# Reordering the lead-in of a two-layer convolution and attention kernel: large loads first, a joint weight product spread over five banks, and the group norm's products placed inside it

## The reference, cut to what matters

```python
def _gn(v, G=32, eps=1e-5):
    g = v.reshape(B_, G, C_ // G, H_, W_)
    m = jnp.mean(g, axis=(2, 3, 4), keepdims=True)
    s = jnp.var(g, axis=(2, 3, 4), keepdims=True)
    return ((g - m) / jnp.sqrt(s + eps)).reshape(v.shape)

# layer 0: depthwise 3x3 convolutions of the normalised image
value = _dwconv(x, w_v, b_v, 1)
query = _dwconv(x, w_q, b_q, 1)
key = _dwconv(x, w_k, b_k, STRIDE)      # stride 2
off = _dwconv(x, w_off1, b_off1, STRIDE)
...
# layer 1
mid = jax.nn.silu(xn @ fc1_w + fc1_b) @ fc2_w + fc2_b
...
o = o + mid
o = o @ proj_w + proj_b

x = x + _L0_conv_ref(_gn(x), ...)
x = x + _L1_conv_ref(_gn(x), ...)
```

## Time and profile before

| | us |
|---|---|
| median of 3 runs | 2768.92 |
| the profiled execution, whole | 2791.05 |
| its span | 2789.2 |
| PE busy | 2687.2 (96%) |
| DVE busy | 1978.9 (71%) |
| ACT busy | 1169.6 (42%) |
| mean granted TensorE clock | 0.969 |

### The profile page before, as it was taken

One profiled execution on the slowest core, in us unless ns is written; L12 is line 12 of the kernel. 1 busy time (PEld: TensorE's weight loads), 2 busy tenths in 40 slices (PEclk: granted clock), 3 DMA queues, 4 the chain that ended last, 5 costly groups with the idle time before them and its releaser, 6 DMA issues.

```text
span 2789.2 us, 36724 instructions
## 1 busy us (share of the span) xinstructions
PE 2687.2 (96%) x14382; PEld 2444.5 (88%) x14382; DVE 1978.9 (71%) x2513; ACT 1169.6 (42%) x2035; POOL 655.7 (24%) x219
## 2 busy tenths in 40 slices
PE   6998799999999999999999999999999999999999
PEld 4556799999998899999998899999998899999998
DVE  4988785988887685988887685988887534434343
ACT  3432465444442465444442366444442253333332
POOL 0020142222232043222223042322224033211210
PEclk8998899999999999999999999999999999999999
DMA  5257643343338642334337743333346632112110
GB/s 224 59 151 246 207 129 83 105 114 114 102 108 258 215 132 75 103 106 115 123 91 231 241 140 84 102 102 102 104 124 204 232 101 70 44 44 57 44 43 30
DMA packets 208249, 345.52 MB, mean 124 GB/s; under 512 B 24272, under 2 KB 191824, under 8 KB 205392
## 3 DMA queue, kind: packets, MB, share of 16 engines
q1 hardware_dynamic: 182048, 309.87, 34.3%
q10 hardware_dynamic: 21552, 14.05, 3.7%
q0 software_dynamic: 4480, 19.27, 2.4%
HBM read 239.59 MB, written 103.56 MB: 123 GB/s over the span
## 4 chain that ended last, share of the span: by engine, by line
PE 74%; DMA 7%; issue 7%; DVE 5%; POOL 4%; ACT 2%; SPq 0%; ACTq 0%; DVEq 0%; POOLq 0%
PE bank L780 16%; PE bank L781 16%; PE bank L782 16%; PE bank L826 3%; PE bank L985 3%; PE bank L987 3%; PE bank L986 3%; PE bank L1008 3%; PE bank L1176 3%; DMA r_scr<-rr 3%; POOL rq L702 2%; PE bank L1162 2%; DVE AC L2391 1%; PE bank L1120 1%; POOL ro L706 1%
## 5 line engine op out<-in xcount | busy, mean ns | idle before, releaser
L1750 ACT ACTIVATE S<-bank,b1p 128x448 f32<-128x448 f32 x336 | 212.4, 632 | 819.5 <-PE bank L782 752.5
L2391 DVE SCALAR_TENSOR_TENSOR AC<-XV,wfold,AC 128x1568 f32<-128x1568 f32 x288 | 530.0, 1846 | 11.5 <-ACT AC L1782 8.9
L780 PE MATMUL bank<-SH,W2H 128*128 128x448 f32 x1008 | 389.9, 387 | 0.2
L780 PE MATMUL bank<-XRH,W1H 128*128 128x448 f32 x1008 | 376.8, 374 | 1.3 <-ACT S L1750 1.3
L781 PE MATMUL bank<-SL,W2H 128*128 128x448 f32 x1008 | 374.0, 371 | 0.0
L782 PE MATMUL bank<-SH,W2L 128*128 128x448 f32 x1008 | 373.7, 371 | 0.0
L781 PE MATMUL bank<-XRL,W1H 128*128 128x448 f32 x1008 | 373.2, 370 | 0.0
L782 PE MATMUL bank<-XRH,W1L 128*128 128x448 f32 x1008 | 371.9, 369 | 0.0
L702 POOL TENSOR_TENSOR rq<-qn,nhalf 112x32 f32<-112x32 f32 x28 | 181.9, 6498 | 481.0 <-DVE qn L2330 481.0
L2360 DVE TENSOR_TENSOR SL<-S,SH 128x448 fp32r<-128x448 f32 x336 | 207.1, 618 | 87.7 <-ACT SH L1753 87.7
L706 POOL TENSOR_TENSOR ro<-on,nhalf 112x32 f32<-112x32 f32 x28 | 180.2, 6434 | 298.7 <-DVE on L2351 298.6
(11 more groups left out here) (227 smaller groups left out, 5169.0 us busy)
## 6 DMA issues: line engine op xcount, KB each, us to landing
XV<-in_xp SPq DMA_DIRECT2D x36, 870.0 KB, 6.9
XC<-in_xp SPq DMA_DIRECT2D x13, 1682.0 KB, 9.2
CQ<-q_scr SPq DMA_DIRECT2D x28, 672.0 KB
CX<-in_x SPq DMA_DIRECT2D x28, 672.0 KB, 5.2
x_scr<-CX SPq DMA_DIRECT2D x28, 672.0 KB, 5.7
X<-x_scr SPq DMA_DIRECT2D x28, 672.0 KB, 4.2
V<-v_scr SPq DMA_DIRECT2D x28, 672.0 KB, 7.3
Y<-x_scr SPq DMA_DIRECT2D x28, 672.0 KB
```

Source lines behind the costliest of these rows:

```text
L780: mm(o, wh, xh, start=first, stop=False)
L1750: fn(S[:, j % 2, :], bank[j % 2][:, 0:T], ACT.Silu, bias=b1p[:, j:j + 1]).then_inc(s["s_s"], 1)
L2391: stt(o, XV[h][:, ky:ky + HR, kx:kx + W], wfold[:, kind, k, 3 * ky + kx:3 * ky + kx + 1], o, ALU.mult, ALU.add).then_inc(s["va"], 1)
```

## The change

It touches the head of the lead-in and one order on DVE.

```diff
         CONSTS = 13
+        WB = (5, 6, 1, 2, 3)
@@ block.sync
+            sp.dma_start(projw[:, :, :].rearrange("p k c -> p (k c)"), d["proj_w"]).then_inc(s["stg_ld1"], 16)
+            sp.dma_start(fc2w[:, :, :].rearrange("p k c -> p (k c)"), d["fc2_wT"]).then_inc(s["stg_ld1"], 16)
+            for k in range(KC):
+                sp.dma_start(XP[k][:, :, :], xpad_v[0, :, k, :, :]).then_inc(s[f"x0_ld{k}"], 16)
+            sp.dma_start(grp[:, :, :], d["grp"]).then_inc(s["grp_ld"], 16)
             for dst, src in [
...
                 sp.dma_start(dst.ap(), src).then_inc(s["const_ld"], 16)
-
-            sp.dma_start(projw[:, :, :].rearrange("p k c -> p (k c)"), d["proj_w"]).then_inc(s["stg_ld1"], 16)
-            sp.dma_start(fc2w[:, :, :].rearrange("p k c -> p (k c)"), d["fc2_wT"]).then_inc(s["stg_ld1"], 16)
-            for k in range(KC):
-                sp.dma_start(XP[k][:, :, :], xpad_v[0, :, k, :, :]).then_inc(s[f"x0_ld{k}"], 16)
-            sp.dma_start(grp[:, :, :], d["grp"]).then_inc(s["grp_ld"], 16)
@@ block.tensor
-            pe.wait_ge(s["const_ld"], CONSTS * 16)
-            pe.wait_ge(s["stg_ld1"], 32)
-            for j in range(JC):
-                if j >= 2:
-                    pe.wait_ge(s["set_lo"], j - 1)
+            def joint_weight(j):
+
+                if j >= len(WB):
+                    pe.wait_ge(s["set_lo"], j - len(WB) + 1)
                 for k in range(KC):
-                    last = mm(bank[5 + j % 2][:, 0:C], fc2w[:, k, j * P:(j + 1) * P], projw[:, k, :],
+                    last = mm(bank[WB[j % len(WB)]][:, 0:C], fc2w[:, k, j * P:(j + 1) * P], projw[:, k, :],
...
+            pe.wait_ge(s["stg_ld1"], 32)
+            for j in range(9):
+                joint_weight(j)
...
-            gn_groups(0, bank[4], bank[7])
+            gn_groups(0, bank[4], bank[7], lambda: joint_weight(9))
+            joint_weight(10)
+            joint_weight(11)
+            pe.wait_ge(s["const_ld"], CONSTS * 16)
@@ front_taps
+                    if m == 0:
+                        pe.wait_ge(s["set_lo"], JC)
@@ block.scalar
-            act.wait_ge(s["const_ld"], CONSTS * 16)
...
+            joint_high(0, 9)
             act.wait_ge(s["kvq_ld"], 16)
             fn(WKVH[:, :, :], kvw[:, :, :], ACT.Copy).then_inc(s["w_h"], 1)
-            fn(WPH[:, :, :], projw[:, :, :], ACT.Copy).then_inc(s["w_h"], 1)
+            joint_high(9, 10)
...
+            joint_high(10, JC)
...
+            act.wait_ge(s["const_ld"], CONSTS * 16)
             act.wait_ge(s["gn_cf"], 2)
-            front_centre(0)
+            front_centre(0, slice(0, 1))
             front_diag(0)
+            front_centre(0, slice(1, 2))
             front_centre(1)
             front_diag(1)
+            fn(WPH[:, :, :], projw[:, :, :], ACT.Copy).then_inc(s["w_h"], 1)
@@ block.vector
-            dve.wait_ge(s["const_ld"], CONSTS * 16)
-            dve.tensor_reduce(wsum[:, :, :], wconv[:, :, :, :], AX.X, ALU.add)
...
-                order = [(k, c, i) for k in range(2) for i in range(1, 9) for c in (1, 0)]
+                order = [(0, c, i) for c in (1, 0) for i in range(1, 9)]
+                order += [(1, c, i) for i in range(1, 9) for c in (1, 0)]
...
-            for j in range(4):
-                w2_low(j)
-            chunk_stats(0)
-            w2_low(4)
-            w2_low(5)
-            chunk_stats(1)
-            w2_low(6)
-            w2_low(7)
-            chunk_stats(2)
+            w2_low(0)
+            chunk_stats(0)
+            w2_low(1)
+            w2_low(2)
+            chunk_stats(1)
+            for j in range(3, 6):
+                w2_low(j)
+            chunk_stats(2)
             dve.wait_ge(s["x0bn"], STRIPS)
-            gn_coefs(0, bank[4], bank[7], ((w2_lows(8, JC),), (wkv_low,), ()))
+            gn_coefs(0, bank[4], bank[7], ((w2_lows(6, 9),), (weight_sums, w2_lows(9, 10), wkv_low), ()))
+            w2_low(10)
+            w2_low(11)
             small_conv(0, 48)
```

More of the change, by code:

```diff
@@ L1372, in _, with joint_high @@
             fn = act.activation
-            act.wait_ge(s["const_ld"], CONSTS * 16)
             def f(ap):
                 return ap.bitcast(F32)
-            for j in range(JC):
-                act.wait_ge(s["set_w2"], j + 1)
-                fn(W2H[:, j, :], bank[5 + j % 2][:, 0:C], ACT.Copy).then_inc(s["stg_h"], 1)
+            def joint_high(first, last):
+                for j in range(first, last):
+                    act.wait_ge(s["set_w2"], j + 1)
+                    fn(W2H[:, j, :], bank[WB[j % len(WB)]][:, 0:C], ACT.Copy).then_inc(s["stg_h"], 1)
+            joint_high(0, 9)
             act.wait_ge(s["kvq_ld"], 16)
             fn(WKVH[:, :, :], kvw[:, :, :], ACT.Copy).then_inc(s["w_h"], 1)
-            fn(WPH[:, :, :], projw[:, :, :], ACT.Copy).then_inc(s["w_h"], 1)
+            joint_high(9, 10)
             act.wait_ge(s["gn_s1"], 1)
@@ L1393, in _, with front_centre @@
                 last.then_inc(s["bord"], 2)
-            def front_centre(k):
+            joint_high(10, JC)
+            def front_centre(k, which=slice(0, 2)):
                 centre = XP[k][:, 1:2 + 2 * (HK - 1):2, 1:2 + 2 * (WK - 1):2]
@@ L1399, in front_centre @@
                     act.wait_ge(s["ktp"], HEAD + 2)
-                for dst, conv, sg in ((OA2[:, k, :], 3, "o0"), (KA2[:, k % 2, :], 2, "k0")):
+                for dst, conv, sg in ((OA2[:, k, :], 3, "o0"), (KA2[:, k % 2, :], 2, "k0"))[which]:
                     fn(dst.rearrange("p (r w) -> p r w", w=WK), centre, ACT.Identity,
@@ L2034, in w2_low @@
                 dve.wait_ge(s["stg_h"], j + 1)
-                tt(W2L[:, j, :], bank[5 + j % 2][:, 0:C], f(W2H[:, j, :]), ALU.subtract).then_inc(s["set_lo"], 1)
+                tt(W2L[:, j, :], bank[WB[j % len(WB)]][:, 0:C], f(W2H[:, j, :]), ALU.subtract).then_inc(s["set_lo"], 1)
             def w2_lows(first, last):
@@ L2096, in centre_columns, with weight_sums @@
                     last.then_inc(s["set_ctr"], 1)
-            for j in range(4):
-                w2_low(j)
-            chunk_stats(0)
-            w2_low(4)
-            w2_low(5)
-            chunk_stats(1)
-            w2_low(6)
-            w2_low(7)
+            w2_low(0)
[4 more added lines that the diff above has]
+            for j in range(3, 6):
+                w2_low(j)
             chunk_stats(2)
             dve.wait_ge(s["x0bn"], STRIPS)
-            gn_coefs(0, bank[4], bank[7], ((w2_lows(8, JC),), (wkv_low,), ()))
+            def weight_sums():
+                dve.wait_ge(s["const_ld"], CONSTS * 16)
+                dve.tensor_reduce(wsum[:, :, :], wconv[:, :, :, :], AX.X, ALU.add)
+            gn_coefs(0, bank[4], bank[7], ((w2_lows(6, 9),), (weight_sums, w2_lows(9, 10), wkv_low), ()))
+            w2_low(10)
+            w2_low(11)
             small_conv(0, 48)
```

## The result

| | changed kernel | kernel before, on the same chip | ratio [95% interval] |
|---|---|---|---|
| first timing | 2759.22 | 2771.17 | 0.9934 [0.9916, 0.9951] |
| again | 2759.14 | 2779.68 | 0.9930 [0.9914, 0.9947] |
| a third time | 2765.31 | 2782.27 | 0.9951 [0.9932, 0.9971] |

The two columns of times are medians. By the ratios the changed kernel is faster by 18.3, 19.5 and 13.6 us in the three comparisons; the intervals run from 8 to 24 us and all hold 17. (The medians differ by 12.0, 20.5 and 17.0. The 2771.17 counts the three runs of the kernel before that I started from; without them its mean is 2776.37 and that of the changed kernel 2757.91, which gives the 0.9934.) I had forecast 9.4. That the median of 2759.22 stands beside my 2759.5 is luck: the kernel before, 2768.92 in the runs that I started from, took 2776 to 2782 beside the changed one.

What follows compares the result with a forecast made beforehand. PE is busy 96% of the span, but the head is bound by PE and DVE waiting in turns. Savings of 9.2 at the statistics and 0.2 later, none lost, take 2768.9 to 2759.5 us; range 2755.5 to 2764.5.

Steps and rivals of the forecast that it cites:

- Transfers, `fc2w`: Head: with large transfers first, `fc2w` is issued at 1.20, 6.12 us earlier, and lands at 10.4 instead of 16.53.
- The first chunk is issued at 1.7 and lands 16.3 later, at 18.0: Head: DVE waits for this image chunk until 18.0, so the statistics are gathered at 33.4 instead of 42.62, saving 9.2.
- PE idle for 3.8, clock at 1.2 GHz: Ahead of the group norm's first product: PE idles 29.6 to 33.4, so that product takes 3.8 and step 9 takes 3.7.
- My rival without a fall: Clock never falls, or falls late: OA at 44.3, 13.0 early, total 2756 to 2758 us; chance 0.15.
- The sum: Whole kernel: 9.2 at the statistics, 0.2 at the products and the centre, 0 lost in the front: 9.4 us.
- Five banks: Joint weight in the head: PE runs steps 0 to 8 by 29.6 without waiting for DVE; two banks would make it wait.
- `kvw` and `fc1w` "issued at the same times as now": Head transfers: still issued at 10.2 and 10.9 behind the constants, landing at 29.4 and 34.9.
- Constants by 26.5: Head transfers: the 13 small constants, behind the large ones, charged 2.6 us and all landed by 26.5.
- The rival of constants in series: Head transfers: the 13 constants go one after another, 25 us, landing at 49; total 2771.7 us; chance 0.03.
- `WKVL` to OA: Head, behind the products: from the end of `WKVL` (2.54 long) to OA's start takes 3.24, as before; OA at 47.85.
- The new order's cost, 1.8, and PE held by DVE at unit 1: Front: DVE's sixteen operations take 17.0 against 15.2; DVE's 1.9 of slack is used up, holding PE to 9.4.
- The front keeps the gain: Front behind the head: PE and DVE both start earlier, so 0 of the head's 9.4 us is lost.

Runs made afterwards that it cites:

- e5: Changed kernel with `kvw` and `grp` issued ahead of the three image chunks, so the chunks land late; single execution 2776.10 us.
- e1: Kernel before, unchanged, profiled a second time; ratio 0.9992 [0.9976, 1.0009].
- e3: Kernel before with only the changed kernel's order of transfers and waits for constants; joint weight, products and DVE's order as before; ratio 0.9967.
- e6: Changed kernel with two banks for the joint weight instead of five; ratio 0.9975 [0.9956, 0.9994].
- e4: Changed kernel with the 13 constants issued ahead of the large transfers; ratio 0.9974 [0.9959, 0.9988].
- e8: Changed kernel with the 13 constants issued behind `kvw` and `fc1w`; single execution 2766.99 us.
- e10: Changed kernel with the old order of `small_conv` and both centre taps ahead of the first diagonals; 2760.39 us, ratio 0.9926 [0.9900, 0.9951].
- e14: Changed kernel with the 13 constants issued behind `kvw` and `fc1w`, second profile; single execution 2748.84 us.

## Why the prediction was wrong

The sign was right, and the gain too small: 9.4 against some 17. By its own steps:

- **Transfers, `fc2w`: right.** Issued at 1.17, landed at 10.06 (10.4).
- **"The first chunk is issued at 1.7 and lands 16.3 later, at 18.0": the step that failed.** It landed at 14.0. The least value of the row belongs to the second chunk. The rate was in the rows already there: `fc2w` itself, and the 12.1 us, from 16.5 to 28.6, in which three chunks followed it. With 14.0 in its place the same sum, low part 0 at 15.4, three chunks at 3.74, five low parts and the gathering, gives 30.7 instead of 33.4. Measured: 29.79 to 30.73. This is 2.7 of the difference. The Trainium skill, "DMA: Bandwidth & Descriptors" (Queues, rings and completion order), says that each DMA engine takes the descriptors of a ring in their order; the three chunks, landing 4.1 apart, agree.
- **PE idle for 3.8, clock at 1.2 GHz: wrong, in part as a consequence.** With 30.7 the idle time is 1.1 by my numbers; it was 0.55 to 0.57. The clock held past the bias sums in all four profiles of the changed kernel. My rival without a fall puts OA at 44.3 where the forecast has 47.85, which gives this term: 3.6. With the chunk late the price came out right (e5). That idle times of 2.05 to 2.80 ahead of a step or a product go with a fall holds in every profile that has one (before, e1, e3, e5, e6). That a short one saves the clock does not: with 0.55 it fell in e4, e8, e10 and e14. So it stays open how much of the 3.6 is the earlier chunk's and how much is that none of the four executions had a late rise. I also misread the windows a little: the clock fell at 43.5 and 53.8 and came back at 67.4, where I have 43.8, 53.9 and 67.2. No term hangs on it.
- **The sum again:** 9.4 + 2.7 + 3.6 = 15.7 at OA, measured 16.1. The taps gain 1.0 more, where I had 0.3: the bias sums end at 44.0, ahead of the diagonals, and do not hold them.
- **Five banks: right in kind.** I said that they let PE run ahead. Without them OA is 3.7 to 6.4 later (e6), by which profiles it is set against: 1.5 to 2.6 at the gathering and the rest at a step that stands ahead of the product, with a fallen clock.
- **`kvw` and `fc1w` "issued at the same times as now": wrong, without effect.** SP was held for 12 us at the constants. The landings (29.0 and 34.5 against 29.4 and 34.9) were right because they follow from the bytes ahead.
- **Constants by 26.5: right** (the last, `woff2c`, was issued at 22.05 and took 4.6). The rival of constants in series is refuted: from the landing of the first, `ident_s`, at 23.8 to that of the last at 26.7 all 13 took 2.9.
- **`WKVL` to OA: right**, 5.85 (5.78).
- **The new order's cost, 1.8, and PE held by DVE at unit 1: right.** 16.9 for sixteen operations, and waits of 0.3 to 1.8.
- **The front keeps the gain: right**, and 1.8 more appear between the taps and `woT`. The first gather on POOL took 1.13 in three profiles of the changed kernel, and 2.65 to 2.75 in its second and in both of the kernel before. Whether that is the cause was not tried, and e8 and e14 differ by 6.8 at this mark with equal taps, so the 1.8 may be no part of the change.
- **The rival "clock never falls, or falls late" was the case**, with a chance of 0.15: it fell at 44.2, ahead of the taps. Its gain at OA, 13.0, was worked out with the late chunk, and so is too small as well.

## What to carry to other kernels

Check a landing time against the rate: transfers of one queue can't land closer together than their bytes allow (16.3 and 18.0 for two chunks issued 0.5 apart would be 1682 KB in 2.2 us, some 780 GB/s, where the highest that any window of 1 us showed is 519), and a median that is the exact middle of the smallest and the largest value is a row with a value missing. Put the transfers that the first engine waits for ahead of the many small ones; behind them the small ones cost nothing as long as their users come later. A step that ends in an idle time of PE can be worth more than its length: by my working the late chunk cost 2.7 by itself and 3.6 by the clock, and e5 has OA 6.5 later than the changed kernel.

## What the runs showed of the hardware that I had not expected

- SP's issuing is held when it runs too far ahead of large transfers. In the changed kernel the first ten transfers are issued in 0.39 to 0.78 each, the eleventh, the second `b`, takes 3.78 (the row above has both `b` together, 4.26), then come 3.44, 3.45 and 2.80, a little less than the 4.1 in which a chunk moves. In e5 the hold begins at the tenth, `hsel_s`, with 2.83, in e14 and e8 at the tenth, `head_s`, with 7.30 and 7.47. In e4 and in the kernel before, where the 13 small ones were issued and mostly landed first and at most eight large ones were under way, nothing was held (0.39 to 0.74). No engine waited for it here; work of SP's own behind such a hold would be 12 us late.
- The clock around the same instructions held or fell between executions (0.53 to 1.00 in one window), for 2.7 us at OA. One profile of a kernel doesn't show which.
- The same head (OA at 44.12 and 44.27) came with times 18 us apart, on two chips, so a gain of this size is read from marks and means, not from one execution.
